# Two edits to a one-core graph network kernel: when edge tiles are loaded, and where operands of layer 1 lie

## The reference

```
h  = relu(layernorm(x))
x1 = x + relu(h @ W_self + mean over edges of h[src] @ W_neigh + b)
h  = relu(layernorm(x1))
e  = sigmoid(relu([h[src], h[dst]] @ We1 + be1) @ We2 + be2)      one number per edge
m  = e * h[src]                                                   64 numbers per edge
h2 = relu([max of m per node, sum of m per node, h] @ Wn1 + bn1)
out = x1 + (h2 @ Wn2 + bn2 + h)
```

## Time and profile before

| | us |
|---|---|
| median of 3 runs | 6236.28 |
| lowest and highest | 6231.25 and 6246.97 |
| profiled execution, its own time | 6239.78 |
| profiled execution, its span | 6238.1 |
| first layer 1 gather to last DVE instruction of the last tile | about 2702 to 6115 |

### The profile page before, as it was taken

One profiled execution on the slowest core, in us unless ns is written; L12 is line 12 of the kernel. 1 busy time (PEld: TensorE's weight loads), 2 busy tenths in 40 slices (PEclk: granted clock), 3 DMA queues, 4 the chain that ended last, 5 costly groups with the idle time before them and its releaser, 6 DMA issues.

```text
span 6238.1 us, 109218 instructions
## 1 busy us (share of the span) xinstructions
PE 3708.8 (59%) x24783; PEld 3315.1 (53%) x24784; DVE 4334.1 (69%) x9411; ACT 1836.3 (29%) x3642; POOL 4293.1 (69%) x3884
## 2 busy tenths in 40 slices
PE   0004866787787788835555555566555666666661
PEld 0003756677777777734445444555555555555551
DVE  5788666666666666646667677677777777787881
ACT  6103655666666666600000000000010001111110
POOL 5245534666766766677777777777777777777777
PEclk9999988899999999955555555555555555555555
DMA  7110111333333333343333333333333333333341
GB/s 237 53 35 11 26 32 42 113 109 104 117 109 105 116 114 107 113 122 97 99 104 97 105 102 104 105 102 109 103 105 108 107 109 107 109 107 115 113 120 29
DMA packets 402218, 611.87 MB, mean 98 GB/s; under 512 B 191933, under 2 KB 274979, under 8 KB 402107
## 3 DMA queue, kind: packets, MB, share of 16 engines
q0 software_dynamic: 182688, 377.75, 21.9%
q1 hardware_dynamic: 150357, 130.12, 6.5%
q10 hardware_dynamic: 69094, 103.21, 5.5%
HBM read 470.99 MB, written 118.43 MB: 94 GB/s over the span
## 4 chain that ended last, share of the span: by engine, by line
POOL 42%; issue 22%; PE 13%; DVE 10%; DMA 6%; DVEq 3%; ACT 2%; SPq 1%; POOLq 1%; ACTq 0%; PEld 0%
POOL counts_f L567 32%; POOL extra_f L567 7%; PE ps_acc L1786 4%; PE ps_pairs L1778 4%; POOL records L589 2%; ACT counts_f L1597 2%; DMA counts_f<-hA_table,stage 2%; PE ps_acc L1855 2%; DMA extra_f<-hA_table,estage 1%; DVE hot L1251 1%; DMA win<-sorted_rows 1%; PE ps_acc L1756 1%; DVEq L469 1%; POOL out_dram L712 1%; DVE pre L1023 1%
## 5 line engine op out<-in xcount | busy, mean ns | idle before, releaser
L567 POOL DMA_INDIRECT counts_f<-hA_table,stage x2496 | 2630.6, 1054 | 771.1 <-issue 762.9
L1756 PE MATMUL ps_acc<-msg,ident 128*128 128x64 f32 (+1 forms) x4974 | 1271.9, 430 | 1300.6 <-DVE msg L1416 1297.9
L1756 PEld LDWEIGHTS ps_acc<-msg,ident 128*128 128x128 f32 x4974 | 1121.6, 326 | 1451.0 <-DVE msg L1416 1165.1
L1597 ACT ACTIVATE counts_f<-ps_pairs 128x784 bf16<-128x784 f32 x1568 | 1268.8, 823 | 714.3 <-PE ps_pairs L1778 657.3
L567 POOL DMA_INDIRECT extra_f<-hA_table,estage x780 | 991.2, 1271 | 242.7 <-issue 242.4
L1778 PE MATMUL ps_pairs<-hot 128*128 128x196 bf16 x6272 | 857.6, 261 | 462.8 <-DVE hot L1251 316.6
L1399 DVE TENSOR_TENSOR pre<-counts_f,own 128x512 f32 (+1 forms) x854 | 594.9, 697 | 704.6 <-SPq L850 541.1
L1786 PE MATMUL ps_acc<-pieces_f,counts_f 128*128 128x192 bf16 x9604 | 1066.1, 254 | 1.7 <-ACT counts_f L1597 1.1
L1684 ACT ACTIVATE gate<-z,be_col 128x4 f32<-128x4 f32 x854 | 253.8, 297 | 2761.0 <-DVE z L1411 2755.7
L1786 PEld LDWEIGHTS ps_acc<-pieces_f,counts_f 128*128 128x128 bf16 x9604 | 923.9, 140 | 4.7 <-issue 2.0
L1778 PEld LDWEIGHTS ps_pairs<-hot 128*128 128x128 bf16 x6272 | 557.9, 101 | 561.2 <-issue 531.3
(11 more groups left out here) (239 smaller groups left out, 2990.6 us busy)
## 6 DMA issues: line engine op xcount, KB each, us to landing
early_rows<-extra_f SPq DMA_DIRECT2D x196, 384.0 KB, 2.9
counts_f<-early_rows ACTq DMA_DIRECT2D x98, 768.0 KB
counts_f<-hA_table,stage POOLq DMA_INDIRECT x2496
counts_f<-counts_f SPq DMA_DIRECT2D x78, 288.0 KB, 2.6
own<-own_rows ACTq DMA_DIRECT2D x98, 128.0 KB
extra_f<-hA_table,estage POOLq DMA_INDIRECT x780
hA_table<-node ACTq DMA_DIRECT2D x98, 96.0 KB, 1.6
sorted_rows<-srt SPq DMA_DIRECT2D x14, 252.0 KB, 2.6
```

What stands on the lines that cost most here:

```text
L567: return pool.indirect_dma_start(to, None, table, bass.IndirectOffsetOnAxis(ap=idx, axis=axis))
L1597: act.activation(counts[:, c, nodes, :].rearrange("p (b h) t -> p b (h t)", h=2), ps_pairs[g & 1][:, :].rearrange("p (b w) -> p b w", b=BA ...
L1756: return pe.matmul(ps_sum[:, 0:D], ident[:, :], rows, start=False, stop=False, skip_group_check=True)
```

## The change

It has two parts that share no instruction.

In layer 0, SP's iteration `q` now loads the edges of pair `q + 1`, between the two loads of node rows and so ahead of the five stores of its own iteration. Three pairs are loaded ahead of the loop (two before), and the last iteration loads none.

In layer 1, `B` of a tile (`ps_b`, by an ACT copy one tile ahead), the gates and `We2` (`ps_we2`, once) are put in PSUM, in banks that layer 0 used for `ps_pairs1`. `pre_act`, `message` and `weigh` read their second operand there. `sums_of` and `finish` leave DVE: ACT copies `h`, the sum and the output, and PE adds `h` and `x1` to the output with two more identity matmuls. ACT's order within a tile becomes: the two copies for the sum, a gate, two copies and the hidden layer, a gate, the output copy (behind the wait for PE's output), the copy of `B`, the two loads, and then the gates of the late chunks. PE's transposes now wait for `s_acc`, and its output for `s_finished`.

```diff
-        ps_pairs = [psum(f"ps_pairs{h}", [P, 2 * BANK]) for h in range(2)]
+        ps_4 = psum("ps_4", [P, 4 * BANK])
+        ps_pairs = [ps_4[:, 2 * BANK * h:2 * BANK * (h + 1)] for h in range(2)]
...
         ps_idx = ps_t[:, 0:P].bitcast(BF16)
+        ps_b = ps_4[:, BANK:3 * BANK].rearrange("p (a w) -> p a w", a=2)[:, :, 0:H]
+        gate = ps_4[:, 3 * BANK:3 * BANK + SLOTS]
+        ps_we2 = ps_4[:, 4 * BANK - H:4 * BANK]
...
                              ebuf[:, e, :, :].rearrange("p k w -> p (k w)")).then_inc(s_ew[e], 16)
-            def next_tiles(q):
-                wait_alone(sp, s_prep, q * 2)
-                for c in range(2):
-                    load_edges(q * 2 + c, c)
-                for c in range(2):
-                    wait_alone(sp, s_x1, q * 2 + (c - 3))
-                    load_nodes(q * 2 + (c - 2), c)
+            def next_tiles(q, edges=True):
+                wait_alone(sp, s_x1, q * 2 - 3)
+                load_nodes(q * 2 - 2, 0)
+                if edges:
+                    wait_alone(sp, s_prep, q * 2 + 2)
+                    for c in range(2):
+                        load_edges(q * 2 + (c + 2), c)
+                wait_alone(sp, s_x1, q * 2 - 2)
+                load_nodes(q * 2 - 1, 1)
...
             for t in range(2, 4):
+                load_edges(t, t & 1)
+            sp.wait_ge(s_prep, 4)
+            for t in range(4, 6):
...
                     store_early(q - 2, e)
-            with in_one_block(sp, 6 + TITER, TPAIRS) as q:
+            with in_one_block(sp, 6 + TITER, TPAIRS - 1) as q:
...
                     store_early(q - 2, e)
+            next_tiles(TPAIRS - 1, edges=False)
+            for e in range(GROUP_PIECES):
+                store_early(TPAIRS - 3, e)
...
                 v.tensor_tensor(pre[:, :, :], rows[:, :, D:WROW],
-                                own_at(i, 0, H).to_broadcast([P, SLOTS, H]), ALU.add).then_inc(s_pre, 1)
+                                ps_b[:, bass.ds(i & 1, 1), :].to_broadcast([P, SLOTS, H]), ALU.add).then_inc(s_pre, 1)
...
                 v.scalar_tensor_tensor(out=act_w[:, :, :], in0=pre[:, :, :], scalar=0.0,
-                                       in1=bc_mid(we2_rows[:, :], SLOTS), op0=ALU.max, op1=ALU.mult).then_inc(s_act, 1)
+                                       in1=bc_mid(ps_we2, SLOTS), op0=ALU.max, op1=ALU.mult).then_inc(s_act, 1)
...
                 v.tensor_tensor(to, run_max[:, :], chunk_max[:, :], ALU.max).then_inc(s_acc, 1)
-            def finish(i):
-                v.wait_ge(l1.y, i + 1)
-                st.link(v.tensor_tensor(last_sum[:, :], ps_y[:, 0:D],
-                                        own_at(i, H + D, H + 2 * D).rearrange("p a b -> p (a b)"), ALU.add))
-                v.tensor_tensor(at_tile(out_ranked, i), last_sum[:, :],
-                                own_at(i, H, H + D).rearrange("p a b -> p (a b)"), ALU.add).then_inc(s_finished, 1)
             def first_chunk(i, before):
-                wait_alone(v, s_own, i * 16 + 16)
+                wait_alone(v, s_second, i + 2)
...
                 pre_act(early_rows_of(i, 1), i)
-                if before_it is not None:
-                    sums_of(before_it)
...
                 beside(w, late_rows(slots_before), early_rows_of(i, ECHUNKS - 1))
-                if before_it is not None:
-                    finish(before_it)
...
                 maximum(last, cat[:, 0:D])
-            def sums_of(i):
-                v.tensor_copy(h_tile[:, :], own_at(i, H + D, H + 2 * D).rearrange("p a b -> p (a b)")
-                              ).then_inc(l1.cat, 1)
-                wait_alone(v, l1.sum, i + 1)
-                v.tensor_copy(cat[:, D:2 * D], ps_sum[:, 0:D]).then_inc(l1.cat, 1)
...
             tile(0, None, 1)
-            first, per = st.now(), 1
             with in_one_block(v, 1, T - 1) as i:
-                st.at(i * per + (first - per))
                 tile(i, i - 1, i + 1)
-                assert st.n == per
-            st.at(first + per * (T - 2))
...
             tile(T - 1, T - 2, None)
-            sums_of(T - 1)
-            finish(T - 1)
...
                     load_early(i, i)
+            def copy_b(i):
+                act.activation(ps_b[:, bass.ds(i & 1, 1), :], own[:, bass.ds(i & 3, 1), 0:H], ACT.Copy
+                               ).then_inc(s_second, 1)
...
                 act.activation(gate[:, :], z[:, :], ACT.Sigmoid, bias=be2_col[:, 0:1]).then_inc(s_gate, 1)
+            def sum_out(i):
+                act.activation(h_tile[:, :], own[:, bass.ds(i & 3, 1), H + D:H + 2 * D].rearrange("p a b -> p (a b)"),
+                               ACT.Copy).then_inc(l1.cat, 1)
+                act.wait_ge(l1.sum, i + 1)
+                act.activation(cat[:, D:2 * D], ps_sum[:, 0:D], ACT.Copy).then_inc(l1.cat, 1)
+            def output_copy(i):
+                act.wait_ge(l1.y, i + 1)
+                act.activation(at_tile(out_ranked, i), ps_y[:, 0:D], ACT.Copy).then_inc(s_finished, 1)
...
                 if before_it is not None:
-                    sum_copies(before_it)
+                    sum_out(before_it)
...
                 if before_it is not None:
+                    sum_copies(before_it)
...
                 gate_of(before + 2)
+                if before_it is not None:
+                    output_copy(before_it)
+                if next_it is not None:
+                    wait_alone(act, s_own, i * 16 + 32)
+                    copy_b(i + 1)
...
                 if own_next:
-                    wait_alone(act, s_own, i * 16 + 32)
...
                     gate_of(before + n)
+            act.activation(ps_we2, we2_rows[:, :], ACT.Copy).then_inc(s_second, 1)
+            act.wait_ge(s_own, 16)
+            copy_b(0)
...
             gates(T - 1, T - 2, False, False, None)
+            sum_out(T - 1)
...
             hidden(T - 1)
+            output_copy(T - 1)
...
                 last.then_inc(s_msgf, 1)
-            def sum_transposes(i):
+            def own_at(i, lo, hi):
+                return own[:, bass.ds(i & 3, 1), lo:hi].rearrange("p a b -> p (a b)")
+            def sum_transposes(i, chunks):
+                wait_alone(pe, s_acc, chunks + 1)
...
                 wait_alone(pe, s_hids, i + 1)
+                wait_alone(pe, s_finished, i + 1)
                 pe.matmul(ps_y[:, 0:D], h2T[:, :], w_n2[:, :], start=True, stop=False)
-                pe.matmul(ps_y[:, 0:D], ones[0:1, 0:P], bn2_row[:, :], start=False, stop=True).then_inc(l1.y, 1)
+                pe.matmul(ps_y[:, 0:D], ones[0:1, 0:P], bn2_row[:, :], start=False, stop=False)
+                pe.matmul(ps_y[:, 0:D], ident[:, :], own_at(i, H + D, H + 2 * D), start=False, stop=False)
+                pe.matmul(ps_y[:, 0:D], ident[:, :], own_at(i, H, H + D), start=False, stop=True).then_inc(l1.y, 1)
...
                 if before_it is not None:
-                    sum_transposes(before_it)
+                    sum_transposes(before_it, before)
...
             tile(T - 2, None)
-            sum_transposes(T - 1)
+            sum_transposes(T - 1, pe.snap(walk.before, min_val=0, max_val=MAXCHUNKS))
```

More of the change, by code:

```diff
@@ L297, in gnn_kernel @@
         z = sb("z", [P, SLOTS])
-        gate = sb("gate", [P, SLOTS])
         msg = sb("msg", [P, SLOTS, D])
@@ L301, in gnn_kernel @@
         run_max = sb("run_max", [P, D])
-        last_sum = sb("last_sum", [P, D])
         win = sb("win", [P, 2, RUN], I32)
@@ L453, in gnn_kernel @@
         s_finished = sem("s_finished")
+        s_second = sem("s_second")
         s_pre = sem("s_pre")
```

## The result

The changed kernel takes **5838.99 us** (median of 4 runs, 5831.75 to 5843.71), and the kernel before 6237.70 beside it (4 runs, 6231.25 to 6246.97). The ratio is **0.936**, with a 95% interval of 0.934 to 0.938: faster by 399 us, where 386 were forecast (5850, range 5745 to 5940).

What follows compares the result with a forecast made beforehand. No engine was taken to bound the whole: POOL's gathers bound layer 1, and layer 0, where DVE waited for edges, would become POOL's. 6239.8 us less 143 and 243 gives 5854, the median 3.5 lower: 5850, range 5745 to 5940.

Steps and rivals of the forecast that it cites:

- Layer 0, edges ahead of stores: Layer 0: DVE's 8.0 us wait goes, POOL then bounds; iterations 38.0 us from 42.1, 35 of them, gain 143 us.
- Rival A: Layer 0 gains all of DVE's wait, 35 x 8.0 = 280 us: 5713 us in all; chance 0.05.
- Gathers released: Layer 1: PSUM operands stop holding POOL's gathers; each takes 950 ns, at a pitch of 1.259 us instead of 1.363.
- the 4 ns kept for the 64-wide instructions: Layer 1: hold per gather still left by 64-wide DVE instructions; without it the gain would be 252 us, not 243.
- Rival C: Layer 1 gathers stay at 1054 ns, held by something else; only layer 0 gains: 6093 us; chance 0.04.
- The cost of a PSUM operand: Layer 1, DVE: three instructions reading PSUM cost 0 to 0.11 us more per chunk, taken as 0.05.
- Rival B: Layer 1: DVE bounds many more tiles, 0.2 us more per chunk, no tile-end gain: 5892 us; chance 0.13.
- D: Rival: half-rate PSUM reads, 1.3 us more per chunk, DVE bounds all layer 1 tiles: 6661 us; chance 0.02.
- The tile's end: Layer 1: of 2.7 us taken off DVE, about 0.5 per tile is kept; bounds 3.1 less to 1 more.
- PE is late next: Layer 1 tile end: PE's output ends at 5862.5 instead of 5861.2, so `message` waits for single-slot sums.
- Who bounds which tiles: Layer 1: DVE bounds the last 11 or so tiles, POOL the rest; they cross at 6.8 chunks per tile.
- The sum of layer 1: 2907 us for 2309 slots, 6 for last rows, 252 for last 11 tiles: 3165 against 3408, gain 243.

Runs made afterwards that it cites:

- e1_edges: Kernel before with only SP's new load order, layer 1 as before: 6097.73 us, ratio 0.976.
- the kernel that was to test it: Changed kernel with every fourth early gather left out (15 instead of 20 per iteration): 7772.37 us, then 7805.64 us, ratio 0.992, on slower chips.
- e6_gate_first: Changed kernel with ScalarE making the first chunk's gate after the output copy before copying B and issuing the two loads, not after: 5822.60 us, ratio 0.932.
- e3_psum_only: Changed kernel with the tile's end back on DVE; three operands in PSUM and new load order stay: 5855.26 us, ratio 0.937.
- e7_gate_sbuf: Changed kernel with the gates in SBUF again, on a slower chip: 7990.11 us, ratio 1.023.
- the four that ran beside one another: e1_edges, e3_psum_only, e6_gate_first and the changed kernel with SP's old order (6001.32 us, ratio 0.960), on one chip with the kernel before.

## Why the prediction was right, point by point

- **Layer 0, edges ahead of stores: right in mechanism and size.** Iterations of 37.8 us for 38.0, 152 us for 143. POOL without a pause, 1.414 us per instruction where 1.434 was read from the earlier trace rows, and DVE in the wait for own rows, 4.8 us per iteration for 5.3. The sum gave the stage 35 iterations of 4.1 us. e1_edges alone gives it too. Rival A, 5713, fell as the earlier trace rows had it: POOL's held time per iteration rose, from 7.6 us to 22 x (1.414 - 0.945) = 10.3. That less of POOL's work would end the wait isn't shown, as the kernel that was to test it ran only on the slower chips.
- **Start and end of the stage: not in the sum.** The first six of these iterations, from 1116 to 1325 us, took 34.4 to 35.5 us, while POOL's scatters stood 37 to 40 us apart: DVE could run ahead of POOL until its lead was used up. So DVE's last `edge_ids` came at 2421.9 instead of 2592.2, 170 us earlier. At the end POOL had that backlog to work off, and the first ring gather came only 152 us earlier: 133 us behind `edge_ids` instead of 115. The sum of equal iterations left out both, and they cancel but for a few us.
- **Gathers released: right.** 946 ns for 950, so the 4 ns kept for the 64-wide instructions weren't needed (10 us of 2496 gathers). Maximum 1021 for 1522. Rival C, 6093, is out: one operand put back brings the hold back. Of the three that hold, `message` counts for little: 24 us in the kernel before. With its operand alone in SBUF some gathers still take up to 1197 ns, but their mean is 948 to 950, on the chips where that ran.
- **The cost of a PSUM operand: the term had the wrong sign.** It was taken as 0.05 us more per chunk, in a range of 0 to 0.11. The three instructions went from 697 to 685 ns, from 684 to 679 and from 420 to 416: 0.02 us less, outside the range. Rival B, 5892, and D, 6661, both rested on this price. The Trainium skill, "VectorE: DVE Perf Modes", section "The TRN2 errata — SBUF-src ops pay a fixed extra latency per instruction", gives 65 ns more per instruction by an estimate from its cycles. The trace doesn't agree, with 4 to 12 ns less; the section's figure is for a source in PSUM, and here only the second of two operands lay there.
- **The Trainium skill's other rule**, "SBUF — State Buffer", section "Who interferes with whom", infers that `tensor_tensor` does not stall descriptor generation. The runs contradict it for indirect gathers with 268 us, and with the pairs above. What the same section states of reads, that an instruction with two SBUF inputs contends with a GpSimd instruction that reads SBUF, agrees: each gather takes its row numbers from `stage`, which lies in SBUF. So the prediction set aside one half of that section, and the other half speaks for its choice. Which part of a gather is held, the reading of row numbers or the writing of descriptors, no run here shows.
- **The tile's end: the step that failed.** "PE is late next", it said, and ACT's order "is hidden behind that". A tile of 7 chunks took 24.4 us (5439.87 to 5464.28) where 24.2 was forecast and 24.7 was before, but it is ACT's gate that is late, 2.0 us per tile, and the closing matmul comes after only when the gate is moved (0.6 us, in 23 tiles). In its example the output ended at 5862.5, the sums and the closing matmul at 5865.1 (2.6 us later) and the gate came 2.9 us later. Measured, PE was done 1.9 us behind the output's end (5446.21 to 5448.11) and the gate began 3.6 us behind it. Two estimates were made to fall together, they were off by 0.7 us in opposite directions, and the text took the cover for real. It had named the price, "it would cost what it is late by", and e6_gate_first got that back: 22.3 us for such a tile.
- **Who bounds which tiles: right in kind, not in number.** A tile of 7 chunks costs DVE 24.6 us with the old end and 22.3 with the gate ahead. Over 98 tiles that is 225 us, and e3_psum_only and e6_gate_first are 33 us apart: POOL's pace takes the rest. But the last 11 or so tiles were to stay DVE's, and in the kernel after it is the last 23. From 5162.6 on every tile of 8 chunks takes 27.3 us and every tile of 7 takes 24.4, and DVE's waits for rows are down to 4.3 us. The sum took POOL's pace for full tiles. Many of these tiles aren't full: with 19 slots where 20 fit, one of 7 chunks takes POOL 19 x 1.25 = 23.8 us, less than DVE.
- **The sum of layer 1: near in part by luck.** It forecast 243 us, and the traces give 255.5 - 9.1 = 246. The terms differ more than the total: 268 us less held time where the 2309 gathers that it counted give 240, then 13 us more idle time of POOL (27 of it more waiting at a full ring, 14 less issue) and a tail 9 us longer, both left out.

Open: what one operand alone is worth in time on the ordinary chip; whether fewer gathers shorten layer 0; and whether the change pays on a chip like the two slower ones, where the kernel after wasn't run itself, and those one edit from it stood at 0.99 to 1.02 of the kernel before.

## What to carry to other kernels

Where GpSimd's gathers are the bound, compare their mean with their median: the gap is held time, and the timeline shows beside which instructions of VectorE it is lost. Giving those instructions one operand in PSUM cost VectorE nothing here and returned all of it. When work moves to another engine, look at what is queued behind it there, and count the stall only in the tiles which that chain bounds.

## What the runs showed of the hardware

- `tensor_tensor` with its second operand in PSUM, over 512 numbers with a repeated row, took 685 ns where both operands in SBUF took 697; `scalar_tensor_tensor` 679 against 684.
- In the kernel before, gathers that start in a 512-wide `tensor_tensor` or `scalar_tensor_tensor` with both operands in SBUF are held for 0.32 and 0.30 us on average, in a 256-wide one for 0.11 us, and in a reduction for nothing. With one of the operands in PSUM none is held.
- The 0.30 us of issue ahead of each ring gather summed to 749 to 766 us in the kernel after and in the four that ran beside one another, whether gathers were held or not.
- On two of the chips the kernel before took a quarter longer (7775 and 7869 us for 6238). DVE's and POOL's instructions had the same length in the kernels that ran there: a free gather 946 to 950 ns, DVE busy 4284 to 4294 us for 4246. Most of the longer time lies between instructions: in layer 1 of e7_gate_sbuf POOL waits 1534 us for its ring. What differs on those chips isn't shown.
